# Two self attentions of a twelve-layer kernel: fp32 products replaced by three products of 12-bit parts

## What is computed

```
h = layernorm(x)                       # 2048 x 256
q, k, v = h @ Wq, h @ Wk, h @ Wv       # each 256 x 1024: 16 heads of 64 (group 2 adds biases)
s = 0.125 * q @ k.T                    # per sequence of 32 tokens and head; causal in group 2
o = softmax(s) @ v
x = x + o @ Wo + bo                    # Wo is 1024 x 256
```

## Time and profile before

| | us |
|---|---|
| median of three runs (lowest, highest) | 3868.98 (3868.51, 3870.46) |
| the profiled execution's own time | 3871.93 |
| its span in the trace | 3870.2 |
| group 2's self attention, first normalisation to last x | 845.3 to 1143.9 |
| group 4's self attention, the same | 3534.0 to 3826.4 |
| PE busy over the span | 3535.6 |

### The profile page before, as it was taken

One profiled execution on the slowest core, in us unless ns is written; L12 is line 12 of the kernel. 1 busy time (PEld: TensorE's weight loads), 2 busy tenths in 40 slices (PEclk: granted clock), 3 DMA queues, 4 the chain that ended last, 5 costly groups with the idle time before them and its releaser, 6 DMA issues.

```text
span 3870.2 us, 89624 instructions
## 1 busy us (share of the span) xinstructions
PE 3535.6 (91%) x38028; PEld 2681.6 (69%) x38028; DVE 2053.5 (53%) x5210; ACT 1229.8 (32%) x3121; POOL 884.4 (23%) x1359
## 2 busy tenths in 40 slices
PE   7988669989997889999999899999999999999996
PEld 6866557546776668777777456767787677777774
DVE  5756642554455165555554566554444466664346
ACT  6853101322112223333333333232232244442111
POOL 6667033230012332222222322100000100101002
PEclk9989679989997989999999999999999999998997
DMA  5610366720012421111110100031221111111000
GB/s 164 183 55 4 100 212 188 242 88 2 2 55 84 93 69 45 46 49 45 45 49 14 53 2 2 3 115 55 66 87 60 37 39 38 39 38 47 2 2 25
DMA packets 207934, 246.23 MB, mean 64 GB/s; under 512 B 18132, under 2 KB 189905, under 8 KB 204593
## 3 DMA queue, kind: packets, MB, share of 16 engines
q1 hardware_dynamic: 200048, 230.27, 18.9%
q0 software_dynamic: 7488, 10.23, 1.5%
HBM read 221.46 MB, written 18.61 MB: 62 GB/s over the span
## 4 chain that ended last, share of the span: by engine, by line
PE 77%; DVE 12%; issue 4%; ACT 3%; POOL 2%; DMA 1%; SPq 0%; ACTq 0%; POOLq 0%; DVEq 0%
PE psum L180 50%; PE psum L3401 10%; PE psum L888 2%; DVE l3x_P L3733 2%; PE psum L860 1%; PE psum L2884 1%; PE psum L3629 1%; PE psum L2985 1%; DVE g_xn L243 1%; PE psum L2953 1%; DVE l3x_V L3716 1%; PE psum L873 1%; POOL l0a_ms L1072 1%; PE psum L2894 1%; PE psum L2885 1%
## 5 line engine op out<-in xcount | busy, mean ns | idle before, releaser
L230 POOL TENSOR_SCALAR g_rs<-g_mv 128x4 f32<-128x4 f32 x40 | 10.7, 268 | 988.0 <-DVE g_mv L278 986.7
L3401 PE MATMUL psum<-l2f_hhi,l2f_whi 128*128 128x512 f32 x512 | 200.8, 392 | 0.0
L3401 PE MATMUL psum<-l2f_hlo,l2f_whi 128*128 128x512 f32 x512 | 199.2, 389 | 0.0
L3401 PE MATMUL psum<-l2f_hhi,l2f_wlo 128*128 128x512 f32 x512 | 199.2, 389 | 0.0
L180 PE MATMUL psum<-l2x_kT,l2x_Qp 128*128 128x257 f32 x768 | 179.2, 383 | 2.6 <-ACT g_xn L3297 2.6
L180 PE MATMUL psum<-g_xn,l2x_tok 128*128 128x384 f32 x512 | 177.7, 489 | 1.4 <-ACT g_xn L3306 1.4
L180 PEld LDWEIGHTS psum<-l2x_kT,l2x_Qp 128*128 128x128 f32 x768 | 142.0, 191 | 21.7 <-issue 3.0
L3447 DVE CAST l2f_hhi<-l2f_tmp 128x512 fp32r<-128x512 f32 x96 | 41.0, 427 | 201.7 <-ACT l2f_tmp L3505 200.6
L180 PEld LDWEIGHTS psum<-g_xn,l2x_tok 128*128 128x128 f32 x512 | 93.3, 190 | 56.9 <-issue 2.6
L289 DVE TENSOR_TENSOR g_x<-g_x,psum 128x256 f32<-128x256 f32 x128 | 53.3, 417 | 145.6 <-PE psum L180 142.4
L3716 DVE COPY l3x_V<-psum 128x512 f32<-128x512 f32 x64 | 44.3, 692 | 159.6 <-PE psum L180 159.6
(11 more groups left out here) (752 smaller groups left out, 9041.8 us busy)
## 6 DMA issues: line engine op xcount, KB each, us to landing
l2f_raw<-L2f_h SPq DMA_DIRECT2D x64, 512.0 KB, 3.6
l0f_w<-L0f_w SPq DMA_DIRECT2D x23, 1024.0 KB
l0x_ctxT<-ctxT SPq DMA_DIRECT2D x64, 257.0 KB, 2.8
l1x_ctxT<-ctxT SPq DMA_DIRECT2D x64, 257.0 KB, 5.6
l0x_ctok<-ctx SPq DMA_DIRECT2D x64, 256.0 KB, 3.1
l1x_ctok<-ctx SPq DMA_DIRECT2D x64, 256.0 KB
l2x_cT<-ctxT SPq DMA_DIRECT2D x64, 256.0 KB, 2.8
l2x_tok<-ctx SPq DMA_DIRECT2D x128, 128.0 KB, 2.9
```

The source lines that it names most:

```text
L3401: t = e.matmul(z, a, b, start=c == 0 and u == 0, stop=c == 7 and u == 2)
```

## The change

It does the following, for both layers:

- `three` makes each product of q, k, v and of the output projection from parts, as hi*hi, lo*hi, hi*lo.
- `Norm` with `lo` writes h transposed as parts: `hi` in `xT_parts` (the bytes of `xT`), `lo` in `xn_parts` (the bytes of `xn`). DVE makes `hi` of the first bank, and both `lo`; ACT makes `hi` of the second.
- Each weight gets a `hi` (ACT) and a `lo` (DVE, over the bytes of the loaded weight). ACT makes the four `hi` behind its part of the norm; DVE makes the `lo` of q, k and v behind its own, and that of o in tick 1.
- `outT` on DVE makes `hi` of its half and the `lo` of both.
- The bias row moves from ahead of the ticks to the end of tick 1 (`row`). The loads of q, k and v go ahead of that of o.
- The norm's banks are taken in the order 6, 4, 2, 0, and a projection waits for the norm's group that it reads (`norm.ready(w, u // 2)`), where before all four groups were waited for.

```diff
+def three(e, out, pairs, start=True, stop=True):
+    return matmuls(e, out, [(a[p], b[q]) for a, b in pairs for p, q in ((0, 0), (1, 0), (0, 1))], start, stop)
...
 class Norm:
-    def __init__(self, K, second=None, first=False):
+    def __init__(self, K, second=None, first=False, lo=None, banks=(0, 2, 4, 6)):
...
-                z = self.banks[g, c] = K.bank[2 * g + c]
+                z = self.banks[g, c] = K.bank[self.at_bank[g] + c]
...
         def evict(g):
             w.wait_ge(self.ps.at(2 * g + 1))
             o, z = K.xT[:, 0, g * 512:(g + 1) * 512], self.banks[g, 0]
-            if self.second is None:
+            if self.lo is not None:
+                e.tensor_copy(self.hi_at(g, 0), z).then_inc(*self.hi_ok.up())
+                w.wait_ge(self.hi_ok.now())
+                w.wait_ge(self.ps.at(2 * g + 2))
+                e.tensor_tensor(self.lo(g, 0), z, self.hi_at(g, 0), ALU.subtract)
+                w.wait_ge(self.ac.at(g + 1))
+                e.tensor_tensor(self.lo(g, 1), self.banks[g, 1], self.hi_at(g, 1), ALU.subtract).then_inc(*self.dv.up())
+            elif self.second is None:
                 e.tensor_copy(o, z).then_inc(*self.dv.up())
...
 class SelfAttention:
...
         def project(i):
...
-            matmuls(e, z[:, 0:256], [(self.oT[i % 2][:, ch, :], self.wo[:, ch, :]) for ch in range(nch)]).then_inc(*self.y_ps.up())
+            o = self.oT[i % 2]
+            if self.parts:
+                w.wait_ge(self.wo_ok)
+                three(e, z[:, 0:256], [([a[:, ch, :] for a in o], [a[:, ch, :] for a in self.wo]) for ch in range(nch)]).then_inc(*self.y_ps.up())
...
         def outT(i):
...
+            e.tensor_copy(o[0][:, :, 2:4, :], self.o_all[:, :, 2:4, :]).then_inc(*self.o_hi.up())
+            w.wait_ge(self.o_hi.now())
+            if i >= 1:
+                w.wait_ge(self.y_ps.at(i))
+            e.tensor_tensor(o[1][:, :, 2:4, :], self.o_all[:, :, 2:4, :], o[0][:, :, 2:4, :], ALU.subtract)
+            w.wait_ge(self.o_act.at(i + 1))
+            e.tensor_tensor(o[1][:, :, 0:2, :], self.o_all[:, :, 0:2, :], o[0][:, :, 0:2, :], ALU.subtract).then_inc(*self.o_dve.up())
...
 def wide_attn(K, pre, bias, eps, scale, keep, brow_name):
...
         def pe(e):
...
-            norm.all_ready(w)
-            w.wait_ge(mark["w"])
-            if bias:
-                z, _ = banks.take(("fold", 0))
...
+            def row(i):
+                if i:
+                    return
+                w.wait_ge(mark["w"])
+                if bias:
+                    w.wait_ge(w_in["o"].at(2))
+                    matmuls(e, take("fold", 0)[0:1, 0:256], [(K.col("L1_attn_V_b", ch), wo[:, ch, :]) for ch in range(8)]).then_inc(*fold_ps.up())
+                    z = take("bias", 0)
+                    w.wait_ge(brow_ok.at(1))
+                else:
+                    z = take("bias", 0)
+                e.matmul(z[:, 0:256], ones[0:1, :], bo[:], start=True, stop=True).then_inc(*bb_ps.up())
...
             def p1(i, part):
                 u = i // 2
+                norm.ready(w, u // 2)
                 for n in quarter(i, part):
-                    w.wait_ge(w_in["qkv"[n // 4]].at(2))
+                    w.wait_ge(w_lo.at(n // 4 + 1))
+                    z, (hi, lo) = take("p", u, n), W["qkv"[n // 4]]
...
         def dve(e):
             w = K.w(e)
             barrier(K, w)
             norm.dve(e, w)
             banks = mark["banks"]
+            for n in range(3):
+                split(e, w, n)
...
         def act(e):
...
             norm.act(e, w)
             banks = mark["banks"]
             w.wait_ge(L("cols").at(0))
+            for n in range(4):
+                w.wait_ge(w_in["qkvo"[n]].at(2))
+                copy_act(e, W["qkvo"[n]][0][:], raw["qkvo"[n]][:]).then_inc(*w_hi.up())
```

More of the change, by code:

```diff
@@ L118, in tile, with shared @@
         return (scope or self.ctx).enter_context(self.nc.sbuf_tensor(f"{self.tag}_{name}", shape, dt))
+    def shared(self, name, shape, scope=None):
+        with ExitStack() as first:
+            parts = self.tile(name + "_parts", shape, F32R, first)
+        return self.tile(name, shape, F32, scope), parts
     def sig(self, name, unit=1, lasting=False):
@@ L202, in all_ready @@
     def all_ready(self, w):
-        w.wait_ge(self.dv.at(4))
-        w.wait_ge(self.ac.at(4))
+        self.ready(w, 3)
     def ready(self, w, g):
@@ L210, in ready, with hi_at, parts @@
         w.wait_ge(self.ac.at(g + 1))
+    def hi_at(self, g, c):
+        return self.K.xT_parts[:, c, g * 512:(g + 1) * 512]
+    def parts(self, c, a, b):
+        g, o = a // 512, a // 512 * 512
+        return self.hi_at(g, c)[:, a - o:b - o], self.lo(g, c)[:, a - o:b - o]
     def pe(self, e, w):
@@ L262, in act @@
             o, z = K.xT[:, 1, g * 512:(g + 1) * 512], self.banks[g, 1]
-            if self.second is None:
+            if self.lo is not None:
+                copy_act(e, self.hi_at(g, 1), z).then_inc(*self.ac.up())
+            elif self.second is None:
                 copy_act(e, o, z).then_inc(*self.ac.up())
@@ L821, in __init__ @@
         self.nm = T("nm", [128, self.NS, 3, 16])
-        self.oT = [T(f"oT{k}", [128, self.nch, 128]) for k in range(2)]
+        if parts:
+            lo = K.tile("oTlo", [128, self.nch, 128], F32R, sc)
+            self.oT = [[K.tile(f"oThi{k}", [128, self.nch, 128], F32R, sc), lo] for k in range(2)]
+        else:
+            self.oT = [[T(f"oT{k}", [128, self.nch, 128])] for k in range(2)]
+        self.parts, self.wo_ok, self.o_hi = parts, None, S("oT_hi")
         if nulls is not None:
@@ L957, in outT @@
                 w.wait_ge(self.y_ps.at(i - 1))
-            o = self.oT[i % 2][:].rearrange("p c (j q) -> p c j q", j=4)
-            e.tensor_copy(o[:, :, 2:4, :], self.o_all[:, :, 2:4, :]).then_inc(*self.o_dve.up())
+            o = [a[:].rearrange("p c (j q) -> p c j q", j=4) for a in self.oT[i % 2]]
+            if not self.parts:
+                e.tensor_copy(o[0][:, :, 2:4, :], self.o_all[:, :, 2:4, :]).then_inc(*self.o_dve.up())
+                return
[6 more added lines that the diff above has]
+            e.tensor_tensor(o[1][:, :, 0:2, :], self.o_all[:, :, 0:2, :], o[0][:, :, 0:2, :], ALU.subtract).then_inc(*self.o_dve.up())
         def total(i):
@@ L1172, in pe, with take @@
             mark["banks"] = banks
-            norm.all_ready(w)
-            w.wait_ge(mark["w"])
-            if bias:
-                z, _ = banks.take(("fold", 0))
[L1177 to L1183, removed]
+            def take(*key):
+                z, prev = banks.take(key)
                 if prev:
@@ L1206, in ready @@
                 u, n = i // 2, i % 2
+                norm.all_ready(w)
                 w.wait_ge(p_act.at(6 * u + 6))
@@ L1210, in ready @@
                         k[u % 2][:, :, n * 128:(n + 1) * 128].rearrange("p c (j k) -> p c j k", j=4), v[u % 4][:, n, :])
-            ticks(16, {(0, "a"): lambda i: p1(i, 0), (0, "b"): lambda i: p1(i, 1), **at.pe(e, w, banks, ready)},
-                  [2, (0, "a"), 6, 7, (0, "b")])
+            ticks(16, {(0, "a"): lambda i: p1(i, 0), (0, "b"): lambda i: p1(i, 1), (1, "row"): row, **at.pe(e, w, banks, ready)},
+                  [2, (0, "a"), 6, 7, (0, "b"), (1, "row")])
         def pool(e):
```

68 lines of the change are left out of this document (43 added, 25 removed).

## The result

| | before | after |
|---|---|---|
| median of six runs each | 3868.74 us (3868.11 to 3881.10) | 3855.51 us (3850.03 to 3862.24) |
| ratio | | 0.996, 95% interval 0.9945 to 0.9975 |
| profiled execution | 3871.93 us | 3856.87 us |

The change makes the kernel 13 us faster, 0.4%. I had forecast 52 us and a range that ends at 3840: the prediction is wrong on the size, by 38.5 us (51.7 less 13.2).

What follows compares the result with a forecast made beforehand. PE was taken to bound the kernel: 69.8 us gained on projections and 6 in the last ticks, less losses at starts, bias row, missed banks and clock, gave -51.7 us, 3820.2 profiled or 3817.3 against the median; range 3806 to 3840.

Steps and rivals of the forecast that it cites:

- What bounds the kernel, and the prices of a product: PE sets the pace in ticks 2 to 15; parts' products cost 0.120 us (256 columns) and 0.227 (512).
- DVE in the ticks: Ticks with output projection: longer `outT` adds 1.3 us a tile, fits DVE's free time; 3 us charged for odd misses.
- Last ticks: After tick 15: DVE takes over at 5.04 us a tick, gain there nil; 3 us a layer gained overall.
- the last two projections: End of a layer's last ticks: the very last two projections run without DVE's added work, 1.1 us gained.
- the waits beside DVE: Last ticks: waits marked issue partly pass beside DVE, counted within the 3 us gained a layer.
- Clock: Start of each layer: PE idles before the first products and loses clock, 1.5 us a layer, 3 in all.
- the bank waits: Start: PE waits for copied banks after the second bank, 1 us in group 2 and 2 in group 4.
- a thin stretch of small products: Earlier trace's last ticks: output projection after it took 5.13 us instead of 3.72, partly at the lower clock.
- Start: Ahead of the ticks: first q product near 860.5 (group 2) and 3549 (group 4); 3.7 and 9.1 us lost.
- The norm's first group: Start: q's product waiting for it alone gains nothing, as the weight's `lo` signal comes behind all four groups.
- DVE sets the ticks: Rival: output projection's bank comes late by all `outT` grew, 1.3 us in ticks 7 to 15; 3847; chance 0.15, wholly or partly.

Runs made afterwards that it cites:

- the other pair of kernels: Second `lo` tile added to the changed kernel, with the wait for the previous output projection left in (ratio 0.9947) against taken out (0.9854).
- the kernel with one line undone: Changed kernel, but first projections wait for all four norm groups again (`norm.all_ready`): 3856.66 us, ratio 0.9948 to the kernel before.

## Why the prediction was wrong

- **What bounds the kernel, and the prices of a product: right.** Starts are 0.120 apart at full clock. The ticks without output projection fell as computed (five of them from 63.1 to 53.7 us), and with two `lo` tiles all of ticks 2 to 15 took 188.2 where I had said about 188.
- **DVE in the ticks: the step that failed.** I wrote that "`outT` becomes three instructions of about 0.65", 1.3 us more a tile, and asked only whether DVE has the time. It has. The diff adds a wait between the first and the second of the three, and I didn't ask what was queued behind it: `total`, which frees a bank, and the release of the PSUM banks that the next values need. In the full ticks this costs 0.6 a tick (15.60 against 14.96 with two `lo` tiles, mean of the 18 ticks with an output projection), of which 0.38 is the wait for `g_x`, 18 times in both layers. I had 3 us for both layers and it is 11.4.
- **Last ticks: the same step again, and dearer.** I priced a tick by the larger of two sums, PE's 4.3 and DVE's 5.04. A tick in which each engine waits for the other within the same tile is the sum of the links, 6.1, at full clock. The forecast was 3 us gained a layer, measured are 6.6 and 13.2 lost. Without the wait, DVE's 5.04 is seen (4.97 to 5.5), but the gain of 3 a layer is not: +0.7 and -0.3. The clock is 0.85 there instead of 0.96 and 0.93, which is where the 1.1 us for the last two projections and the waits beside DVE may have gone; no run shows it. Of the 19.4 us that the wait costs in the last ticks, 10.7 are waits for `lo`, 3.3 idle time marked issue, and 5.5 a longer busy PE for the same products, the lower clock.
- **Clock: the size near at the start, the place missed.** I charged 1.5 a layer at the start. In group 2 PE ran its first 5.2 us of products at half clock; that costs 2.6 us and ate the bank waits that I had listed, and the stretch came out at +5.4, with +6.3 forecast. What I had not costed was the clock of the last ticks. I had put the 5.13 us of the earlier trace rows down to a thin stretch of small products; PE had also stood idle for 1.82 us just before.
- **Start:** the first product begins 15.35 us after the norm's start in both layers, where I had 15.2 (860.5 and 3549.2). In group 4 that is 6.8 later than before, and the stretch came out 2.2 better than forecast. **The norm's first group** is worth nothing, as said.
- **Rivals.** "DVE sets the ticks" has the sign and a nearby time (3847), with a mechanism that isn't this one: it is not the length of `outT` but its place behind the projection. With the wait taken out, the forecast of -51.7 us against the kernel before stands beside -57.8 and -53.9 by medians, and -50.3 in the two layers. That nearness is partly luck: the last ticks gain nothing where I had 6 us, and the starts lose 4 us less than I had.

In sum the wait costs 30.8 us of the two layers, 11.4 in ticks 2 to 15 and 19.4 in the last ticks (the other pair of kernels gave 34.8). The 0.9 that the start differs by is not its doing: group 2's start is 38.8 to 40.0 us in the traces with DVE's first order, with the wait or without it.

## What to carry to other kernels

When a change adds a buffer beside a doubled one, look whether it is doubled too: one `wait` for "the reader of the last round is done" costs nothing in the sum of instructions and can tie two engines into one chain. Taken out, it gave more here (31 us) than the whole change had given (13). Price a pipelined tick by its longest cycle through all engines and buffers, and not by its busiest engine. Where PE stands still for part of each tick, look at its granted clock too: here the clock took 5.5 of the 19.4 us that the wait costs in the last ticks. A wait made finer is worth something only if nothing else on the same path comes later.

## What the runs showed of the hardware

- Behind the norm's transpositions and 4.90 us without work PE's first products of parts, 256 columns wide, started 0.213 apart, and 0.120 apart from 5.2 us later on. 0.213 is 256 columns at 1.2 GHz. The Trainium skill, "TensorE: Matmul & The Clock Gate", section "Wait — 56ns, not 53.3ns?", gives the distance at the low clock as columns divided by 1.2 GHz, and the trace agrees. For the full clock it gives columns divided by 2.4 GHz and 2.5 ns on top, which makes 0.109 as an estimate; here it is 0.120 in a stream of them, as in the earlier trace rows, so the measured price was the one to use.
- The low clock isn't a matter of starts alone: in the last ticks of group 4, with waits of 1.54 us and idle times marked issue of 0.63 and 2.35 us, windows of 5 us show a granted clock of 0.50. Three laps of 6.1 us with the same wait of 1.54 us and no other idle time ran at 1.00.
- The part of the kernel that no run changed took between 3267 and 3283 us in the nine traces of changed kernels (span less the two layers). A comparison of single executions would have shown differences of that size that no edit made; the two layers' lengths summed to 542.5 and 542.6 us in the two traces of one kernel. With the wait in they are less steady: 574.3 and 569.9 us for the change and the kernel with one line undone.
